# A transformer block on one core: the stages behind attention placed half a group earlier, and two groups of heads in one bank of the sums

## The reference

```
qkv = x @ c_attn_w + c_attn_b                  # 128 -> 3*128, 16 heads of 8
attn = softmax(causal(q k^T / sqrt(8)))        # 512 x 512 for each head
heads 0, 1, 2: attn *= mult (1.6 in one third of the keys), normalised again
x1 = layernorm(x + (attn v) @ c_proj_w + c_proj_b)
h = s0 * [x1, -x1] @ W0;  h = 2 relu(h)        # 128 -> 512
h = s1 * h @ W1;          h = 2 relu(h)        # 512 -> 512
out = layernorm(x1 + s2 * h @ W2)              # 512 -> 128
```

## Time and profile before

| | |
|---|---|
| median of 3 runs | 1000.81 us (995.29 to 1002.84) |
| time of the profiled execution | 994.16 us |
| its span | 992.4 us |
| mean granted TensorE clock | 0.928 |
| PE busy | 864.0 us (87%) |
| DVE busy | 671.9 us (68%) |
| ACT busy | 605.0 us (61%) |
| POOL busy | 502.6 us (51%) |

### The profile page before, as it was taken

How to read it: one execution, slowest core, us unless ns; L and a number is a source line. 1 busy time by engine, 2 the same in 40 slices (tenths; PEclk the granted TensorE clock), 3 DMA queues, 4 the chain that set the end, 5 groups by cost and what they waited for, 6 DMA issues and landing times.

```text
span 992.4 us, 17320 instructions
## 1 busy us (share of the span) xinstructions
PE 864.0 (87%) x5824; PEld 439.0 (44%) x5824; DVE 671.9 (68%) x2784; ACT 605.0 (61%) x1106; POOL 502.6 (51%) x625
## 2 busy tenths in 40 slices
PE   2349698999999899989999998989999898999866
PEld 1114244545454454545454453545455454535343
DVE  3367578575867768595967669595857769694234
ACT  2106467566766667576757667576756767576733
POOL 1103145637564654647574664646565655547540
PEclk8558899979999997999999799999989999999887
DMA  3653635345453534455443435455443425300000
GB/s 77 68 76 60 71 51 69 45 71 56 52 63 46 74 45 66 53 71 60 53 63 45 66 45 75 49 71 59 57 54 50 70 34 73 38 23 2 23 11 11
DMA packets 66142, 53.19 MB, mean 54 GB/s; under 512 B 4518, under 2 KB 64006, under 8 KB 66054
## 3 DMA queue, kind: packets, MB, share of 16 engines
q1 hardware_dynamic: 65190, 51.30, 40.2%
q10 hardware_dynamic: 864, 0.79, 0.3%
HBM read 9.24 MB, written 4.19 MB: 14 GB/s over the span
## 4 chain that ended last, share of the span: by engine, by line
PE 51%; DVE 23%; POOL 9%; ACT 5%; DMA 5%; issue 4%; SPq 2%; ACTq 1%; POOLq 0%; DVEq 0%
PE av_ps L882 10%; DVE max_ps L643 10%; PE max_ps L825 10%; PE score_ps L849 8%; PE bank_ps L909 5%; POOL h_lo L432 5%; PE bank_ps L910 5%; PE bank_ps L808 4%; PE bank_ps L955 3%; DMA stack<-rowmaxT 3%; DVE stats L712 3%; POOL h_hi L430 2%; DMA stack<-parts 2%; DVE rowmax L643 2%; PE bank_ps L944 2%
## 5 line engine op out<-in xcount | busy, mean ns | idle before, releaser
L643 DVE CUSTOM_DVE_ANT_0 max_ps<-max_ps,future 128x512 f32<-128x512 f32 (+3 forms) x1024 | 480.3, 514 | 232.7 <-PE max_ps L825 229.6
L516 ACT ACTIVATE e<-score_ps 128x512 f32<-128x512 f32 x640 | 365.1, 595 | 187.7 <-PE score_ps L849 184.5
L825 PE MATMUL max_ps<-stack 72*128 72x512 bf16 (+3 forms) x1024 | 260.5, 318 | 59.9 <-DVE rowmax L643 36.1
L849 PE MATMUL score_ps<-stack 75*128 75x512 bf16 (+3 forms) x1024 | 253.8, 310 | 20.8 <-DMA stack<-rowmaxT 16.1
L423 POOL TENSOR_SCALAR_AFFINE_SELECT e<-e 128x512 f32<-128x512 f32 x256 | 160.2, 646 | 129.7 <-ACT e L516 129.7
L882 PE MATMUL av_ps<-e,vaug 128*9 128x512 f32 (+3 forms) x2048 | 194.3, 453 | 3.1 <-ACT avT L523 1.7
L825 PEld LDWEIGHTS max_ps<-stack 72*128 72x128 bf16 x1024 | 83.5, 101 | 218.0 <-DVE rowmax L643 98.3
L432 POOL TENSOR_TENSOR h_lo<-full,h_hi 128x512 fp32r<-128x512 f32 x120 | 153.4, 1278 | 10.0
L508 ACT ACTIVATE full<-bank_ps,scales 128x512 f32<-128x512 f32 x128 | 86.8, 687 | 114.3 <-PE bank_ps L910 93.1
L643 DVE DVE_READ_ACCUMULATOR2_ANT rowmax<- 128x1 f32 x1024 | 143.2, 140 | 0.0
L849 PEld LDWEIGHTS score_ps<-stack 75*128 75x128 bf16 x1024 | 90.1, 100 | 78.7 <-issue 23.8
(11 more groups left out here) (83 smaller groups left out, 791.6 us busy)
## 6 DMA issues: line engine op xcount, KB each, us to landing
stack<-parts SPq DMA_DIRECT2D x288, 128.0 KB
x_in<-in_L_attn_hidden_states SPq DMA_DIRECT2D x16, 256.0 KB, 5.7
x_res<-in_L_attn_hidden_states SPq DMA_DIRECT2D x16, 256.0 KB, 11.4
out_x<-res SPq DMA_DIRECT2D x16, 256.0 KB, 10.9
stack<-rowmaxT ACTq DMA_DIRECT2D x32, 24.0 KB
e<-in_L_ffn_k SPq DMA_DIRECT2D x1, 256.0 KB, 3.5
wc<-in_L_attn_c_attn_w SPq DMA_DIRECT2D x1, 192.0 KB
e<-in_L_ffn_k SPq DMA_DIRECT2D x1, 128.0 KB, 3.3
```

The source lines that it names most:

```text
L516: nc.scalar.activation(e[g % 2][:, t, :], score_ps[:, t % 2, :], ACT.Exp, scale=SCALE).then_inc(exped, 1)
L643: return nc.vector.tensor_tensor_reduce(out=scored_block, in0=scored_block, in1=future[:, P * (T - 1 - qt):S], scale=1.0, scalar=NEG, op0= ...
L825: return nc.tensor.matmul(out_ap[:, col:col + width], st[0:QK_ROWS, h, 0, P * qt:P * qt + P], st[0:QK_ROWS, h, 1, 0:width], start=True, st ...
L849: return nc.tensor.matmul(out_ap[:, col:col + width], st[0:ALL_ROWS, h, 1, P * kt:P * kt + P], st[0:ALL_ROWS, h, 0, P * kt:S], start=True, ...
```

## The change

1. `PLACES` is written anew. `proj` goes from (2, 6) to (2, 0), `x1T` from (3, 2) to (2, 5), `ffn0` from group 3 to the end of group 2 and (3, 0). `ffn1_0` and `ffn1_1` are made at (3, 6) and (3, 8) of the same iteration, `ffn1_2` and `ffn1_3` at (0, 0) and (0, 2) of the next. The four pairs of `ffn2T` are at (0, 4) to (0, 7), one a step, and `ffn2` is at (0, 9) right behind `v`.
2. Two groups of heads share `av_ps`. `vaug` holds two heads in 34 columns: the even one's 9, zeros, and the odd one's 9 from column 25. A product of the even group takes columns 0 to 24 and one of the odd group columns 9 to 33, so it is 25 wide, and the odd group's lands 16 partitions lower and is accumulated. `avT` is copied twice an iteration instead of four times, and the 16 turnings of `tok` become 8, in two banks.
3. The high parts of `ffn0_2` and `ffn0_3` are made by VectorE, not POOL. POOL's order is changed with the places.
4. The statistics, moments and norms have steps of their own (`LN_STATS`, `LN_VAR`, `LN_OUT`). SP loads `x_res` behind the taking of `rowmax0` and stores the output after that.

```diff
 PLACES = (
-    ("ffn1_0", -2, (0, 4), (0, 4)),
-    ("ffn1_1", -2, (0, 4), (0, 4)),
-    ("ffn1_2", -2, (0, 6), (0, 6)),
+    ("ffn1_2", -2, (0, 0), (0, 1)),
+    ("ffn1_3", -2, (0, 2), (0, 3)),
+    ("ffn2T", -2, (0, 4), (0, 8)),
     ("v", 1, (0, 7), (0, 8)),
-    ("ffn1_3", -2, (0, 9), (0, 9)),
+    ("ffn2", -2, (0, 9), (0, 9)),
     ("xT", 2, (0, 9), (0, 9)),
     ("q", 2, (1, 0), (1, 1)),
     ("k", 2, (1, 1), (1, 2)),
-    ("tok_0", -1, (1, 2), (1, 2)),
-    ("tok_1", -1, (1, 3), (1, 3)),
-    ("rowmax1", 0, (1, 4), (1, 4)),
-    ("tok_2", -1, (1, 5), (1, 5)),
-    ("tok_3", -1, (1, 6), (1, 6)),
-    ("ffn2T", -2, (1, 8), (2, 0)),
-    ("ffn2", -2, (2, 2), (2, 3)),
-    ("attnT", -1, (2, 3), (2, 3)),
-    ("proj", -1, (2, 6), (2, 6)),
-    ("x1T", -1, (3, 2), (3, 2)),
+    ("rowmax1", 0, (1, 3), (1, 3)),
+    ("tok_0", -1, (1, 4), (1, 4)),
+    ("tok_1", -1, (1, 5), (1, 5)),
+    ("attnT", -1, (1, 7), (1, 7)),
+    ("proj", -1, (2, 0), (2, 0)),
+    ("x1T", -1, (2, 5), (2, 5)),
+    ("ffn0_0", -1, (2, 7), (2, 7)),
+    ("ffn0_1", -1, (2, 8), (2, 8)),
+    ("ffn0_2", -1, (2, 9), (3, 0)),
+    ("ffn0_3", -1, (3, 0), (3, 2)),
     ("rowmax0", 1, (3, 3), (3, 4)),
-    ("ffn0_0", -1, (3, 5), (3, 5)),
-    ("ffn0_1", -1, (3, 5), (3, 5)),
-    ("ffn0_2", -1, (3, 8), (3, 8)),
-    ("ffn0_3", -1, (3, 9), (3, 9)),
+    ("ffn1_0", -1, (3, 6), (3, 7)),
+    ("ffn1_1", -1, (3, 8), (3, 9)),
 )
-FFN2_STEPS = ((1, 8), (1, 8), (1, 9), (1, 9))
+FFN2_STEPS = ((0, 4), (0, 5), (0, 6), (0, 7))
...
+HIGH_ON_POOL = ("ffn0_0", "ffn0_1", "ffn1_0", "ffn1_1", "ffn1_2", "ffn1_3")
...
-LN_VAR = ((2, 7), (2, 3))
-LN_OUT = (((3, 0), (3, 0), (3, 0), (3, 0)), ((2, 7), (2, 7), (2, 7), (2, 7)))
+LN_STATS = ((2, 1), (1, 0))
+LN_VAR = ((2, 2), (1, 9))
+LN_OUT = (((2, 3), (2, 3), (2, 4), (2, 4)), ((3, 2), (3, 3), (3, 4), (3, 5)))
...
+                if live(n + 1):
+                    wait_free(sp, use_of(n + 1, "rowmax0"))
                 if live(n):
                     ...
                     sp.dma_start(x_res[:], x_tok[n.times(1)]).then_inc(xres_loaded, 16)
+                if live(n + -2):
+                    store(n + -2)
...
+                low(1, 1)
+                low(1, 2)
                 masks(0, 0)
+                low(1, 3)
...
+                rstd_of_layer(0)
+                masks(2, 0)
                 rstd_of_layer(1)
+                low(0, 0)
+                low(0, 1)
+                masks(2, 1)
+                low(0, 2)
+                masks(2, 2)
+                low(0, 3)
+                masks(3, 0)
+                low(1, 0)
                 masks(3, 1)
                 masks(3, 2)
...
-            nc.scalar.activation(avT[:, g, :], av_ps[:], ACT.Copy).then_inc(av_out, 1)
+            nc.scalar.activation(avT[:, pair, :], av_ps[:], ACT.Copy).then_inc(av_out, 1)
...
+                for o in range(2):
+                    last = nc.vector.tensor_tensor(
+                        va[:, :, :, ODD * o:ODD * o + R], src[:, :, :, o, :],
+                        bias[:, :, o, :].unsqueeze(1).broadcast_to([P, T, HALF, R]), ALU.add)
...
-                    last = nc.tensor.matmul(av_ps[32 * j:32 * j + R + 1, P * kt:S],
-                                            vaug[b.parity][:, kt, G * g + j, :], src,
-                                            start=(order == 0), stop=(order == 3))
+                    vals = vaug[b.parity][:, kt, head(g, j) // 2, (R + 1) * odd:(R + 1) * odd + ODD]
+                    last = nc.tensor.matmul(av_ps[32 * j:32 * j + ODD, P * kt:S], vals, src,
+                                            start=(order == 0 and not odd), stop=(order == 3 and odd == 1))
```

More of the change, by code:

```diff
@@ L121, in block_kernel @@
     HALF = H // 2
+    SLOT, ODD = 16, 25
     MAX_RING = 3
@@ L265, in ahead, with head @@
             return (n, 3) if g == 0 else (n + 1, g + -1)
+        def head(g, j):
+            return HALF * (g // 2) + 2 * j + g % 2
+        highs_of_dve = [w for w in HIGH_STEPS if w not in HIGH_ON_POOL]
+        HIGHS_OF_DVE = len(highs_of_dve)
         def last_batch(b):
@@ L427, in high_and_low_part @@
             def high_and_low_part(b, layer, m):
[L428 to L433, removed]
+                what, k = f"ffn{layer}_{m}", 1 + FT * layer + m
+                hi, whole = h_hi[layer][:, m, :], full[:, full_slot(b, k), :]
+                if what in HIGH_ON_POOL:
+                    wait_free(pool, use_of(b, what))
+                    nc.gpsimd.tensor_copy(hi, whole).then_inc(hi_by_pool, 1)
+                    per = len(HIGH_ON_POOL)
+                    pool.wait_ge(hi_by_pool, b.times(per, HIGH_ON_POOL.index(what) + 1))
+                else:
+                    pool.wait_ge(hi_by_dve, b.times(HIGHS_OF_DVE, highs_of_dve.index(what) + 1))
+                nc.gpsimd.tensor_tensor(h_lo[layer][:, m, :], whole, hi.bitcast(F32),
+                                        ALU.subtract).then_inc(split_ready, 1)
             def rstd_of(b, i):
@@ L517, in exp, with sums_out @@
                                      scale=SCALE).then_inc(exped, 1)
[L519 to L522, removed]
-                nc.scalar.activation(avT[:, g, :], av_ps[:], ACT.Copy).then_inc(av_out, 1)
+            def sums_out(b, pair):
+                act.wait_ge(summed, b.times(G, 2 * pair + 2))
+                if pair == 0 and b.c > 0:
+                    wait_full(act, use_of(b + -1, "tok_1"))
+                nc.scalar.activation(avT[:, pair, :], av_ps[:], ACT.Copy).then_inc(av_out, 1)
             def activation_out(b, k, what, func, **kw):
@@ L617, in _ @@
             for i in range(2):
-                last = nc.vector.tensor_copy(vaug[i][:, :, 0:3, R:R + 1], mult[:].unsqueeze(3))
+                nc.vector.memset(vaug[i][:, :, :, R:R + 1], 1.0)
+                last = nc.vector.memset(vaug[i][:, :, :, ODD + R:ODD + R + 1], 1.0)
+            last.then_inc(setup_step, 1)
+            dve.wait_ge(setup_step, 5)
+            for i in range(2):
+                nc.vector.tensor_copy(vaug[i][:, :, 0:2, R:R + 1], mult[:, :, 0:3:2].unsqueeze(3))
+                last = nc.vector.tensor_copy(vaug[i][:, :, 0:1, ODD + R:ODD + R + 1], mult[:, :, 1:2].unsqueeze(3))
             last.then_inc(setup_step, 1)
@@ L866, in sums @@
                         pe.wait_ge(v_ready, b.times(1, 1))
-                    if not (b.c == 0 and g == 0):
-                        pe.wait_ge(av_out, b.times(G, g))
+                    if g % 2 == 0 and not (b.c == 0 and g == 0):
+                        pe.wait_ge(av_out, b.times(2, g // 2))
                 elif order == 1:
@@ L895, in rowmax_transposes, with token_transposes @@
                 last.then_inc(bank_full[u[0]], 1)
[L897 to L900 removed]
+            def token_transposes(b, k):
+                if k == 0:
+                    pe.wait_ge(av_out, b.times(2, 2))
+                transposes(use_of(b, f"tok_{k}"), [avT[:, pair, P * t:P * t + P]
+                                                   for t in (2 * k, 2 * k + 1) for pair in range(2)])
             def ffn(b, what, pairs, splits=()):
```

114 lines of the change are left out of this document (54 added, 60 removed).

## The result

The changed kernel takes 1030.63 us (1028.49 to 1032.51), the one before 1001.28: a ratio of 1.0304 [1.0255, 1.0352], slower by 3%. Its profiled execution has 1028.49 us, a span of 1026.5, a mean clock of 0.881 (0.928 before); PE is busy for 885.5 us, POOL for 484.4, ACT for 591.2.

A forecast was written before the change was run, and what follows sets the result against it. TensorE's own work was taken as the bound. Per iteration, 50.6 us of work, 4.7 of waits and 2.3 of clock falls made 57.6 against 55.8, +27 us over 15: 1021, put at 1022 us, own range 1008 to 1050.

The forecast's parts named there:

- The wait at `x1T`: At (2, 5), TensorE waits 2.6 us for the norm's chain of 7.0 us, in one piece.
- The clock: A fall behind the `x1T` wait in four of five iterations, 2.9 us each: 2.3 us in the mean.
- The full-clock iteration: An iteration without a fall takes 55.3 us: 50.6 of TensorE's own work plus 4.7 of waits.
- The border of 1.3 us: At `x1T`, a wait under about 1.3 us means that the clock never falls.
- TensorE's own work: Per iteration, 51.2 - 1.0 + 0.2 + 0.2 = 50.6 us.
- The 0.2 for the wider loads: In the 16 sets of sums, one 25-column load of each shows, 14 ns longer: 0.2 us an iteration.
- its forecast 0.8: The shared bank: two `tok` banks fewer save 1.0 us an iteration, wider loads cost 0.2.
- 0.2 more: The `ffn2T` pairs, alone at their steps, have two more dearer starts: 0.2 us an iteration.
- The other waits: Waits at `ffn2` 0.85, `q` 0.35, `ffn0_0` 0.6, the mask of (3, 3) 0.3, other places 0.1 us.
- The upper bound for `q`: At (1, 0), a wait of 1.4 us at the worst, if POOL is at work during the product with `mult`.
- Tail and head: Tail -5 us from fewer banks of `ffn1` and `tok`; setup 1 us more, once.
- The faster rival: Norm's chain overlaps better, clock never falls, 53.6 us an iteration, 962 to 970 us in all; chance 0.27.

The follow-up runs named there:

- the twelve extra matmuls: The changed kernel with 12 spare matmuls of 512 columns ahead of `x1T`; 1021.05 us, ratio 1.0163.
- the chain put together again: The changed kernel with `LN_STATS` at (2, 0), `LN_VAR` at (2, 1) and all four pieces of `LN_OUT` at (2, 3); 1007.15 us, ratio 1.0045.
- Part 2 alone: The kernel before, in its own places, with only the sharing of one bank by two groups of heads; 1008.09 us, ratio 1.0076.
- the third: The changed kernel with the norm's steps together, six extra matmuls at `x1T`, products with `mult` on POOL and `ffn2T` a step earlier; 997.19 us, ratio 0.9877.

## Why the prediction was right

1030.6 against 1022 forecast: slower, and by the mechanism named. The sum came near in part by luck, since some of its terms are off in opposite ways. By its steps:

- **The wait at `x1T`** (2.6 forecast) is 2.96 us, its chain 6.83 (7.0). `proj` ends at 495.9, so the way from there to the turning is 7.5 us (7.4 forecast), with 4.5 us of own work in it (4.5): the wait is their difference, and only the 0.3 us taken off for the drain and rounding was wrong. That it sets the clock is shown by the twelve extra matmuls, that the norm's new steps lengthen it by the chain put together again (1.43). This is the main cause: that edit alone gives back some 2.6% of the 3%. Of the change's four parts it is thus the norm's steps, not the new places or the shared bank, that cost most.
- **The clock.** Four iterations in five were forecast, every one it was. One fall costs less than 2.9 us: 58.0 against 55.6 to 56.3 at full clock (in the run with twelve extra matmuls) is 1.7 to 2.4, because the half clock absorbs the other waits; where it absorbs none, a fall of 6.8 us costs 3.1 (58.0 against 54.9). The full-clock iteration is 0.3 to 1.0 us longer than the 55.3 forecast. The errors nearly cancel: 57.6 forecast, 58.0 measured.
- **The border of 1.3 us was wrong.** Waits of 0.98 and 0.45 us made the clock fall in some iterations and not in others, and 1.43 left it up in iteration 6. No size of a single wait divides the two here. In the three runs with falls at (3, 3), all 12 of them came behind both waits, and none in the 12 iterations in which the second, 0.45 us, was missing; but 15 iterations had both and no fall.
- **TensorE's own work** (50.6 forecast) was mis-sized. It is 49.9 us in the one undisturbed iteration shown (the norm's steps put together, iteration 6), 1.4 less than before and not 0.6 (iteration 12 has the same). The trace may miss some records, so this is no better than a few tenths. The 0.2 for the wider loads was right: 14 ns a load, and one of them shows in each of the 16 sets. Part 2 alone gives 0.6 of its forecast 0.8 (1.0 less 0.2). So the remaining 0.8 us lies in the new places, for which 0.2 more had been forecast; no run shows which of them.
- **The other waits.** `ffn2` 0.92 (0.85). `q` nothing, with 0.17 at the maximum before it (0.35). `ffn0_0` and the mask nothing in the changed kernel itself; with the clock held, 0.84 (0.6) and 0.98 (0.3). The last was too small by far, and the 0.45 us for the row maxima behind it was overlooked. The upper bound for `q`, 1.4 us if the product with `mult` meets POOL, wasn't reached, since POOL was idle when the products ran; where they met POOL (`ffn2T` a step earlier) the wait was 1.96, and it stood at the maximum ahead of `q`.
- **Tail and head**: -5.7 (-5) and +2.0 (+1).
- **The faster rival** (962 to 970 without falls) was too hopeful. With no fall and no wait over 0.84 us, 982.8 is what is there, and an iteration of 54.9 us, not 53.6: 49.9 of own work, 2.2 of extra matmuls where waits stood, and the smaller waits.
- **Expectations missed.** The first eight runs came out 6 us better (the kernel before with extra matmuls) to 66 us worse than expected. Most took one wait away and left the rest as they were in the sum; these had been hidden, or a collision of VectorE and POOL took their place. The last four came within 7 us (989.7 for the third).

Why (1, 8) waits in part 2 alone, the trace shows, though no run tried it. Its scores wait for an exponential that ScalarE reaches only after issuing the transfer of `rowmaxT` (0.73 us) and making its piece of the splitting of `q` and `k` (1.06):

```profile
537.95 0.73 ACTq L558 DMA_DIRECT2D stack<-rowmaxT  x1
...
538.73 1.06 ACT L612 ACTIVATE parts<-qk 128x1024 bf16<-128x1024 f32 x1 [0.77 <-DVE rowmaxT L705]
```

POOL's piece of that splitting had ended at 537.58. The kernel before has the same two on ScalarE, equally long, but TensorE fills `tok_2` and `tok_3` meanwhile.

## What to carry to other kernels

Where TensorE's clock falls behind a wait, fill the wait with spare matmuls first: it tells what the fall costs, and it brought 2% here, while the moved stages, with the norm's steps together, the products on POOL and ten extra matmuls, came to the same time. Moving the steps of a chain that crosses engines further apart lengthens it, and can turn several short waits into one long one. Before a removed wait is counted as won, read what VectorE's small instructions meet on POOL in their new place.

## What the runs showed of the hardware

- **A small VectorE instruction waits for POOL's whole one.** A product of 128x32 took 0.19 us with POOL idle and 1.28 us beside POOL's 1.26; a cast of 128x32 0.18 and 1.25. Cutting one product in two paid that twice. The maxima, which have only one input in SBUF, kept their 0.42 us beside a mask. The Trainium skill ("SBUF — State Buffer", on who interferes with whom) states that a VectorE instruction with two inputs in SBUF contends with a GpSimd instruction that reads SBUF, one with at most one such input doesn't, and that casts can run in modes that use both pairs of ports, where the engine that comes second is blocked for the whole instruction. The trace agrees, down to the common end. So the price of the smallest instruction is set by the POOL instruction that it meets, not by its own size.
- **The same waits halve the clock in one iteration and not in the next.** 0.98 and 0.45 us with a set of sums between them were followed by 6.8 us at 0.50 in four iterations of one execution (the norm's steps together, six extra matmuls, the products on POOL), and by none in eight others of the iterations 2 to 14. Short gaps are enough, but don't always do it.
- **Extra matmuls of 1.8 us an iteration shorten the program by 2%.** They stand where TensorE waited anyway (54.9 us an iteration with them, 54.7 to 54.9 before where no fall came), and they prevent falls of 2.9 us each.
